# Routing ranks of a mixture-of-experts layer from bfloat16 ones and zeros

## The chip, the cores and the metric

The kernel runs on one core of one Trainium2 chip, as one program in one launch. The metric is the device time of that launch in microseconds (us), the median of several runs. Lower is better. The engines are TensorE (PE in the profile, PEld for its weight loads), VectorE (DVE), ScalarE (ACT), GpSimd (POOL) and SyncE (SP, which here only issues transfers).

## The reference

The input is x, 8 sequences of 512 tokens with 128 channels, so 4096 tokens, all in float32. Three layers follow, each added to x:

```
x = x + 0.5 * ffn(layernorm(x))
x = x + wkv6(layernorm(x))          # a recurrence with a decay per channel
x = x + 0.5 * ffn(layernorm(x))     # the same weights as the first

def ffn(x):
    x = x + attention(layernorm(x, w, b))          # 16 heads of 8 channels
    h = layernorm(x, w2, b2)
    logits = h @ gate_w + gate_b                    # 8 experts
    one_hot = onehot(argmax(logits))
    y = sum over e of one_hot[:, e] * (gelu(h @ w1[e]) @ w2[e])    # hidden size 512
    return x + y
```

Only one expert counts for each token. The kernel therefore sorts the tokens by expert and computes that expert alone.

## The kernel before, in words

The program is a chain of phases. Each is a block in which every engine has its own list of instructions, and between two phases stands a barrier of all engines (`Phase.__exit__`, L63). A feed-forward layer has four phases: the products for queries, keys and values (`qkv_phase`), the attention (`attention_phase`), projection and routing (`project_phase`, the one touched here), and the experts (`expert_phase`). Between the two feed-forward layers stand two phases for the recurrence; at the end the last sum is stored. So `project_phase` runs twice.

`project_phase` walks over 8 slices (SL) of 4 tiles (ST) of 128 tokens. In words, for slice j:

- TensorE: `turn_y(j)` transposes the attention's result (L916), ScalarE copies it to `yT` (L968), `project(j)` multiplies it by `w_proj` (L908).
- VectorE: `add(j)` makes `x1` (L999), `moments_of` and `gather_moments` its mean and variance (L1009, L1017), `variance(j)` adds eps (L1024), `halve(j)` (L1003) updates `x_all`.
- GpSimd: `scale(j)` raises the variance to the power -0.5 (L1162). VectorE: `norm(j)` writes the normalised tokens into `rows` (L1030).
- TensorE: `turn_h(j)` transposes them (L933), ScalarE makes `h2T` (L974), `gate(j)` multiplies by the gate's weights (L924).
- VectorE: `logits`, `greatest`, `equals`, `numbers`, `first`, `choose` (L1037 to L1060) find the first expert with the greatest logit and write a row of 8 zeros and ones per token, `one_hot` (L1060).
- TensorE: `rank(j)` (L941, L943) counts for each token how many tokens before it chose each expert. The first matmul has a triangle of ones as its weights (`below`, 128x128) and all five groups of `one_hot` as its moving operand (40 columns; the fifth group is zero). Four more have a matrix of ones as weights and 32, 24, 16 and 8 columns; each adds the counts of an earlier tile to the later ones, in the same 40 columns of PSUM.
- VectorE: `places(j)` (L1069, L1071) adds the running count of the slices before, `own_places`, `slots` and `whole` (L1076 to L1084) make from it the row to which each token goes.
- GpSimd: `scatter(j)` (L1155) issues four indirect DMAs, one per tile, which write the 128 rows of a tile to their places in DRAM (`sorted`).

These steps are laid out by hand in turns k. In turn k TensorE does `project(k-1)`, `turn_y(k)`, `gate(k-4)`, `turn_h(k-3)`, `rank(k-5)`, in this order. VectorE does `add(k-1)`, `logits(k-4)`, `moments_of(k-1)`, `greatest`, then `places(k-5)`, which waits for the rank of the same turn; after it come `gather_moments(k-1)`, `own_places`, `equals`, `slots`, `variance(k-1)`, `halve`, `numbers`, `whole`, `norm(k-2)`, `first` and `choose(k-4)`. GpSimd does `scale(k-1)` and then `scatter(k-6)`. Engines take their instructions in order, so on GpSimd `scale(5)` of turn 6 stands in front of the first `scatter`, and `scale(6)` and `scale(7)` stand in front of the next two groups of four.

When the last slice has been counted, VectorE stores where each expert's rows end (`pad_row`, L1123), SyncE writes a tile of padding behind each expert's rows (L896), VectorE finds expert and first row of each of 40 tiles of sorted rows (L1124 to L1144), and GpSimd waits for the landing of all 32 scatters. Then comes the barrier. `expert_phase` loads the sorted tiles (L1203) and runs two layers of the expert's weights over each (L1226, L1232, L1239).

All operands of `rank` are float32 before the change. In the trace each of these float32 matmuls shows as two rows for the weight load and two for the matmul.

Of the kernel before, what the change touches and what calls it, by code (L numbers as in the profile page):

```python
# [6 lines left out]
BF16 = mybir.dt.bfloat16  # L7
# [6 lines left out]
P = 128  # L14
# [17 lines left out]
E, HID = 8, 512  # L32
# [5 lines left out]
ST = NT // SL  # L38
# [4 lines left out]
def own(nc, name):  # L43

    return f"{name}_{nc.next_id()}"
# [801 lines left out]
def project_phase(nc, ps, s, x_all, z_all, rows, expert, first_row, xs):  # L847
# [4 lines left out]
    with Phase(nc) as ctx:  # L852
        def sb(name, shape, dt=F32):
            return ctx.enter_context(nc.sbuf_tensor(own(nc, name), shape, dt))

        def sem(name):
            return ctx.semaphore(name)

        def sbs(name, shape, dt=F32):
            return [sb(f"{name}{i}", shape, dt) for i in range(2)]  # L860
# [2 lines left out]
        x1 = [sb(f"x1{i}", [P, ST, P]) for i in range(3)]  # L863
        stats, moments = sb("stats", [P, ST, 6]), sbs("moments", [P, ST, 2])
        power, var, rstd = sb("power", [P, ST]), sbs("var", [P, ST]), sbs("rstd", [P, ST])
        power_set, var_ready, rstd_ready = sem("power_set"), sem("var_ready"), sem("rstd_ready")
        index, base = sb("index", [P, E]), sb("base", [P, E])
        logit, best, equal = sb("logit", [P, ST, E]), sb("best", [P, ST]), sb("equal", [P, ST, E])
        one_hot, place, run = sbs("one_hot", [P, ST + 1, E]), sb("place", [P, ST, E]), sbs("run", [P, E])
        slot_f, slot = sb("slot_f", [P, ST]), sb("slot", [P, NT], I32)  # L870
        total, above, tiles, ends, delta = (sb("total", [P, E]), sb("above", [P, E, NT]), sb("tiles", [P, E]),
                                            sb("ends", [P, E]), sb("delta", [P, E]))
# [11 lines left out]
        psR = [ps[:, 6 + i, 2 * ST * E:(3 * ST + 1) * E] for i in range(2)]  # L884
# [5 lines left out]
        with nc.Block() as block:  # L890
            @block.sync
            def _(sp):
                sp.wait_ge(pads_ready, 1)
                for e in range(E):
                    row = sp.value_load(pad_row[0:1, e:e + 1], min_val=0, max_val=E * (TOK + P) - P)
                    sp.dma_start(xs[ds(row, P), :], s["padding"][:, 0, :]).then_inc(padded, 16)  # L896
                sp.wait_ge(padded, 16 * E)

            @block.tensor
            def _(pe):  # L900
                t = nc.tensor

                def project(j):
                    pe.wait_ge(y_kept, j + 1)
                    if j >= 2:
                        pe.wait_ge(x1_ready, j - 1)
                    for q in range(ST):
                        last = t.matmul(psP[j % 2][:, q * P:(q + 1) * P], yT[j % 2][:, q * P:(q + 1) * P], s["w_proj"][:],  # L908
                                        start=True, stop=True)
                    last.then_inc(projected, 1)  # L910

                def turn_y(j):
                    if j >= 2:
                        pe.wait_ge(y_kept, j - 1)
                    for q in range(ST):
                        last = t.transpose(psY[j % 2][:, q * P:(q + 1) * P], rows[:, j * ST + q, 0:P], s["ident"][:])  # L916
                    last.then_inc(y_turned, 1)

                def gate(j):
                    pe.wait_ge(h_kept, j + 1)  # L920
                    if j >= 2:
                        pe.wait_ge(ranks_read, j - 1)
                    for q in range(ST):
                        last = t.matmul(psL[j % 2][:, q * E:(q + 1) * E], h2T[j % 2][:, q * P:(q + 1) * P], s["gate_w"][:],  # L924
                                        start=True, stop=True)
                    last.then_inc(gated, 1)

                def turn_h(j):
                    pe.wait_ge(normed, j + 1)
                    if j >= 2:  # L930
                        pe.wait_ge(h_kept, j - 1)
                    for q in range(ST):
                        last = t.transpose(psH[j % 2][:, q * P:(q + 1) * P], rows[:, j * ST + q, 0:P], s["ident"][:])  # L933
                    last.then_inc(h_turned, 1)

                def rank(j):


                    hot = one_hot[j % 2][:].rearrange("p t e -> p (t e)")
                    pe.wait_ge(one_hot_ready, j + 1)  # L940
                    t.matmul(psR[j % 2], s["below"][:], hot, start=True, stop=False)  # L941
                    for back in range(1, ST + 1):
                        last = t.matmul(psR[j % 2][:, back * E:], s["ones"][:], hot[:, 0:(ST + 1 - back) * E],  # L943
                                        start=False, stop=(back == ST))
                    last.then_inc(ranked, 1)

                for k in range(SL + 5):
                    if 1 <= k <= SL:
                        project(k - 1)
                    if k < SL:  # L950
                        turn_y(k)
                    if 4 <= k < SL + 4:
                        gate(k - 4)
                    if 3 <= k < SL + 3:
                        turn_h(k - 3)
                    if 5 <= k:
                        rank(k - 5)
# [189 lines left out]
            @block.gpsimd  # L1147
            def _(pool):
                g = nc.gpsimd

                def scatter(j):
                    pool.wait_ge(normed, j + 1)
                    pool.wait_ge(placed, j + 1)
                    for i in range(j * ST, (j + 1) * ST):
                        pool.indirect_dma_start(xs, bass.IndirectOffsetOnAxis(ap=slot[:, i:i + 1], axis=0),  # L1155
                                                rows[:, i, :], None).then_inc(scattered, 16)

                def scale(j):
                    pool.wait_ge(var_ready, j + 1)
                    if j >= 2:  # L1160
                        pool.wait_ge(normed, j - 1)
                    g.tensor_tensor(rstd[j % 2][:], var[j % 2][:], power[:], ALU.pow).then_inc(rstd_ready, 1)  # L1162

                g.memset(power[:], -0.5).then_inc(power_set, 1)
                pool.wait_ge(power_set, 1)
                pool.wait_ge(numbered, 1)
                for k in range(1, SL + 6):
                    if k <= SL:
                        scale(k - 1)
                    if k >= 6:  # L1170
                        scatter(k - 6)
                pool.wait_ge(scattered, 16 * NT)
# [798 lines left out]
def program(nc, d, out):  # L1971
    with Phase(nc) as ctx:
# [15 lines left out]
        def ffn(load=None):  # L1988

            with ExitStack() as inner:  # L1990
                v_all = inner.enter_context(nc.sbuf_tensor(own(nc, "v_all"), [P, NT, H, DK + 1], F32))
                qkv_phase(nc, ps, s, x_all, z_all, v_all, qd, kd, load)
                attention_phase(nc, ps, s, v_all, y_all, qd, kd, load)
            project_phase(nc, ps, s, x_all, z_all, rows, expert, first_row, xs)
            expert_phase(nc, ps, s, expert, first_row, xs, ys)
# [54 lines left out]
```

## Time and profile before

| what | us |
|---|---|
| median of 3 runs | 1562.1 (1561.02 to 1567.3) |
| the profiled execution | 1553.92 |
| its span, first to last instruction | 1552.0 |
| TensorE busy | 1284.2 (83% of the span) |
| VectorE busy | 1082.9 (70%) |
| ScalarE busy | 859.3 (55%) |
| GpSimd busy | 659.1 (42%) |
| first `project_phase`, first instruction to the first load of the experts | 440.4 to 520.2 |
| second one | 1365.4 to 1445.0 |
| mean granted clock of TensorE | 0.871 of 2.4 GHz |

The shares of busy time are means over all phases. To read a change inside one phase, its own stretch has to be cut out; times in the rows are counted from the start of the span. In a list in order of time a row is: start, busy time, engine, line, operation, what it writes and reads, how many instructions it merges, and in brackets how long the engine sat idle before it and what ended that.

### The profile page before, as it was taken

The numbers are of one execution on the slowest core, as the hardware profiler recorded it, in microseconds if no ns is written. First come the engines' busy times: TensorE is split into PE (matmuls) and PEld (weight loads), VectorE is DVE, ScalarE is ACT, GpSimd is POOL, SyncE is SP. The second block draws the span as 40 slices with busy tenths as digits, with TensorE's granted clock in tenths as the row PEclk, the third lists the DMA queues.
The fourth block names the chain that finished last, engine by engine and source line by source line (L and its number), as shares of the span: only waits on it lengthen the run. The fifth ranks groups of instructions, "written<-read, shape, count | busy, mean of one in ns | idle before, by whom it ended". The sixth has DMA issues, their size and how long they took to land. (4 is left out here: it accounts for less than half of the span.)

```text
span 1552.0 us, 39914 instructions
## 1 busy us (share of the span) xinstructions
PE 1284.2 (83%) x12720; PEld 729.3 (47%) x12721; DVE 1082.9 (70%) x1864; ACT 859.3 (55%) x1750; POOL 659.1 (42%) x767
## 2 busy tenths in 40 slices
PE   5499999999978595288789747499999999976693
PEld 3244444444368595135445444234444444376693
DVE  8588888888555233668788758688888888464232
ACT  3178888888831352234334414178888888820451
POOL 4323333333337463355566533323333333337462
PEclk9689999999975797589899958599999999965797
DMA  5513342221001222000000004311111111001124
GB/s 181 152 37 82 91 108 57 54 52 47 16 1 42 60 67 64 14 2 2 3 3 2 3 1 190 83 43 51 48 50 47 50 48 51 7 1 59 53 69 119
DMA packets 81640, 81.93 MB, mean 53 GB/s; under 512 B 16265, under 2 KB 53868, under 8 KB 81536
## 3 DMA queue, kind: packets, MB, share of 16 engines
q1 hardware_dynamic: 72704, 70.01, 16.3%
q0 software_dynamic: 4608, 8.44, 1.6%
q10 hardware_dynamic: 4224, 2.10, 0.5%
q8 instruction: 64, 1.05, 0.3%
q14 instruction: 40, 0.33, 0.1%
HBM read 50.56 MB, written 29.93 MB: 52 GB/s over the span
## 5 line engine op out<-in xcount | busy, mean ns | idle before, releaser
L817 DVE TENSOR_REDUCE maxima<-ps 128x2 f32<-128x1024 f32 x512 | 624.2, 1226 | 91.0 <-PE ps L646 86.4
L799 ACT ACTIVATE probs<-ps 128x512 f32<-128x512 f32 x1024 | 553.2, 593 | 90.4 <-PE ps L673 73.1
L646 PE MATMUL ps<-k_stack,q_stack 62*128 62x512 f32 x1024 | 387.6, 478 | 35.6 <-DMA k_stack<-k_split 24.4
L673 PE MATMUL ps<-q_stack,k_stack 64*128 64x512 f32 x1024 | 392.1, 461 | 0.4
L683 PE MATMUL ps<-probs,v_stack 128*32 128x256 f32 x4096 | 329.0, 393 | 1.1 <-ACT probs L799 1.0
L612 POOL TENSOR_TENSOR inv<-o_rows,minus_one 128x16 f32<-128x16 f32 x64 | 186.0, 2906 | 237.5 <-ACT o_rows L780 237.5
L646 PEld LDWEIGHTS ps<-k_stack,q_stack 62*128 62x128 f32 x1024 | 158.7, 194 | 229.9 <-issue 116.5
L673 PEld LDWEIGHTS ps<-q_stack,k_stack 64*128 64x128 f32 x1024 | 160.1, 187 | 17.0 <-issue 6.8
L683 PEld LDWEIGHTS ps<-probs,v_stack 128*32 128x32 f32 x4096 | 81.1, 108 | 172.6 <-issue 113.1
L1297 POOL DMA_INDIRECT expert_out<-yt,number x80 | 78.3, 979 | 68.1 <-POOL number L1293 34.2
L1274 DVE COPY w_now<-w 128x512 f32 x80 | 34.3, 429 | 85.9 <-issue 42.8
L1255 ACT ACTIVATE xT<-ps,ln_b,ln_w 128x128 f32<-128x128 f32 x80 | 36.6, 457 | 94.4 <-PE ps L1226 94.4
L1232 PE MATMUL ps<-xT,w_now 128*128 128x128 f32 x640 | 88.2, 283 | 0.0
L1239 PE MATMUL ps<-w,hidT 128*128 x640 | 84.5, 276 | 0.0
L1232 PEld LDWEIGHTS ps<-xT,w_now 128*128 128x128 f32 x640 | 80.6, 198 | 0.2
L605 POOL CAST neg_wide<-maxima 128x16 fp32r<-128x16 f32 x64 | 12.6, 196 | 158.7 <-DVE maxima L817 158.7
L1239 PEld LDWEIGHTS ps<-w,hidT 128*128 128x128 f32 x640 | 77.9, 192 | 0.1
L1155 POOL DMA_INDIRECT sorted<-rows,slot x64 | 62.3, 973 | 18.3 <-issue 15.9
L1260 ACT ACTIVATE hidT<-ps 128x512 f32<-128x512 f32 x80 | 47.8, 597 | 36.7 <-PE ps L1232 36.7
L1703 POOL TENSOR_TENSOR r_kx<-r_kx,r_k_factor 128x512 f32<-128x512 f32 x48 | 61.3, 1277 | 12.9 <-PE ps L1881 9.1
L1684 POOL TENSOR_TENSOR r_mixed<-r_shift,zT 128x512 f32<-128x512 f32 x40 | 56.9, 1431 | 18.0 <-DVE r_shift L1560 18.0
L1226 PE MATMUL ps<-ident,xt 128*128 128x128 f32 x80 | 23.3, 292 | 44.2 <-DMA xt<-sorted 44.1
(205 smaller groups left out, 1765.5 us busy)
## 6 DMA issues: line engine op xcount, KB each, us to landing
q_stack<-q_split SPq DMA_DIRECT2D x256, 64.0 KB
k_stack<-k_split SPq DMA_DIRECT2D x512, 32.0 KB
q_split<-q_parts SPq DMA_DIRECT2D x16, 512.0 KB, 2.7
k_split<-k_parts SPq DMA_DIRECT2D x16, 512.0 KB, 3.4
xt<-sorted SPq DMA_DIRECT2D x80, 64.5 KB
w<-in_L_ffn_w SPq DMA_DIRECT2D x16, 256.0 KB, 3.1
rows<-expert_out SPq DMA_DIRECT2D x16, 256.0 KB, 3.3
x_all<-in_L_attn_x SPq DMA_DIRECT2D x8, 256.0 KB, 3.1
```

Of the source, the lines that this page charges most:

```text
L612: g_.tensor_tensor(inv[:], o_rows[:, :, :, DK], minus_one[:], ALU.pow).then_inc(inv_ready, 1)
L646: mm = t.matmul(psS[:, h, :], qs[g][score_rows(h), h // 2, u * P:(u + 1) * P], ks[g][score_rows(h), h // 2, :], start=True, stop=True)
L673: t.matmul(ring("e", u, n), ks[g][half(h), h // 2, u * P:(u + 1) * P], qs[g][half(h), h // 2, :], start=True, stop=True).then_inc(e_ready, 1)
L683: last = t.matmul(psO[VW * h:VW * (h + 1), here], vs[g][:, u, h, :], probs[u % 2][:, h, here], start=(u == 0 and part == 0), stop=(u == TP ...
L799: a.activation(probs[u % 2][:, h, :], ring("e", u, n), ACT.Exp, scale=float(DK) ** -0.5).then_inc(e_read, 1)
L817: v.tensor_reduce(maxima[i][:, :, pair, u:u + 1], psS[:, 2 * pair:2 * pair + 2, :], AX_X, ALU.max, negate=True).then_inc(s_read, 1)
L1155: pool.indirect_dma_start(xs, bass.IndirectOffsetOnAxis(ap=slot[:, i:i + 1], axis=0), rows[:, i, :], None).then_inc(scattered, 16)
L1232: last = t.matmul(psH[o][:, c * P:(c + 1) * P], w1_now[o][:, c * P:(c + 1) * P], xT[o][:], start=True, stop=True)
L1239: last = t.matmul(psY[i][:, 0:P], hidT[i][:, c, :], s["w2"][:, ds(second_expert, 1), c, :], start=(c == 0), stop=(c == HC - 1))
L1297: pool.indirect_dma_start(ys, bass.IndirectOffsetOnAxis(ap=number[out_slot][:], axis=0), yt[out_slot][:], None, bounds_check=TOK - 1, oob_ ...
L1684: g.tensor_tensor(mixed[f][:], shift[f % 2][:], x, ALU.add).then_inc(mixed_ready.sem, 1)
L1703: g.tensor_tensor(dst[:].rearrange("p (k m) -> p k m", m=m), src[:].rearrange("p (k m) -> p k m", m=m), k_factor[l][:].rearrange("p n two ...
```

## The change

`below` and `ones` get copies in bfloat16, `one_hot` becomes bfloat16, and `rank` takes these three. The sums stay float32 in PSUM. All values are zero or one. GpSimd makes the two copies at the start of each `project_phase`, between its memset of `power` and `scale(0)`, and TensorE waits for both before the first rank.

```
+        counters_set = sem("counters_set")
-        one_hot, place, run = sbs("one_hot", [P, ST + 1, E]), sb("place", [P, ST, E]), sbs("run", [P, E])
+        one_hot, place, run = sbs("one_hot", [P, ST + 1, E], BF16), sb("place", [P, ST, E]), sbs("run", [P, E])
+        below, ones = sb("below_16", [P, P], BF16), sb("ones_16", [P, P], BF16)
...
                     pe.wait_ge(one_hot_ready, j + 1)
-                    t.matmul(psR[j % 2], s["below"][:], hot, start=True, stop=False)
+                    if j == 0:
+                        pe.wait_ge(counters_set, 2)
+                    t.matmul(psR[j % 2], below[:], hot, start=True, stop=False)
                     for back in range(1, ST + 1):
-                        last = t.matmul(psR[j % 2][:, back * E:], s["ones"][:], hot[:, 0:(ST + 1 - back) * E],
+                        last = t.matmul(psR[j % 2][:, back * E:], ones[:], hot[:, 0:(ST + 1 - back) * E],
                                         start=False, stop=(back == ST))
...
                 g.memset(power[:], -0.5).then_inc(power_set, 1)
+                g.tensor_copy(below[:], s["below"][:]).then_inc(counters_set, 1)
+                g.tensor_copy(ones[:], s["ones"][:]).then_inc(counters_set, 1)
                 pool.wait_ge(power_set, 1)
```

## Rows read from the trace of the kernel before

**Rows 1.** Waits of 440 to 520: waiting engine, tile, releaser: total, times, longest.

```profile
DVE place L1069 <- PE ps L943: 14.4, 7, 2.5
```

**Rows 2.** Groups of POOL's instructions, 440 to 515: count, busy, mean ns, idle before.

```profile
L1155 POOL DMA_INDIRECT sorted<-rows,slot x32 | 31.2, 975 | 9.2 <-issue 7.9 <-DVE slot L1084 0.6 <-DVE rows L1030 0.3
```

**Rows 3.** POOL in order of time: the last scales and the scatters around them.

```profile
446.61 1.28 POOL L1162 TENSOR_TENSOR rstd<-var,power 128x4 f32<-128x4 f32 x1 [6.08 <-DVE var L1024]
...
469.09 1.50 POOL L1162 TENSOR_TENSOR rstd<-var,power 128x4 f32<-128x4 f32 x1 [5.26 <-DVE var L1024]
470.67 1.21 POOL L1155 DMA_INDIRECT sorted<-rows,slot  x1
...
476.24 1.49 POOL L1162 TENSOR_TENSOR rstd<-var,power 128x4 f32<-128x4 f32 x1 [0.58 <-DVE var L1024]
...
481.73 0.96 POOL L1155 DMA_INDIRECT sorted<-rows,slot  x1 [0.30 <-issue]
482.74 1.28 POOL L1162 TENSOR_TENSOR rstd<-var,power 128x4 f32<-128x4 f32 x1
```

**Rows 4.** The end of the first phase and the start of the experts, in order of time.

```profile
505.12 0.20 DVE L1144 SCALAR_TENSOR_TENSOR first_row<-counts,row_f 128x40 int32<-128x40 f32 x1
...
513.40 0.95 POOL L1155 DMA_INDIRECT sorted<-rows,slot  x1 [0.31 <-issue]
520.16 2.59 SPq L1203 DMA_DIRECT2D xt<-sorted  x3
```

**Rows 5.** TensorE and VectorE in turns 5 and 6, in order of time.

```profile
459.94 0.30 PEld L941 LDWEIGHTS ps<-one_hot,below 128*128 128x128 f32 x2
461.06 1.46 PEld L908 LDWEIGHTS ps<-w_proj,yT 128*128 128x128 f32 x8
...
462.93 1.11 DVE L1030 TENSOR_SCALAR rows<-x,moments,rstd 128x128 f32<-128x128 f32 x4
...
464.81 0.90 PEld L933 LDWEIGHTS ps<-ident,rows 128*128 128x128 f32 x4
465.21 0.19 DVE L1037 TENSOR_TENSOR logit<-ps,gate_b 128x32 f32<-128x32 f32 x1 [0.24 <-PE ps L924]
...
465.70 0.55 PEld L941 LDWEIGHTS ps<-one_hot,below 128*128 128x128 f32 x2
...
468.09 0.19 DVE L1069 TENSOR_TENSOR place<-ps,run 128x32 f32<-128x32 f32 x1 [1.82 <-PE ps L943]
...
468.85 0.16 DVE L1024 TENSOR_SCALAR var<-moments 128x4 f32<-128x4 f32 x1
```

**Rows 6.** VectorE in turn 7 of the first phase: the variance.

```profile
476.00 0.16 DVE L1024 TENSOR_SCALAR var<-moments 128x4 f32<-128x4 f32 x1
```

**Rows 7.** The same places in the second phase, in order of time.

```profile
1393.05 0.19 DVE L1069 TENSOR_TENSOR place<-ps,run 128x32 f32<-128x32 f32 x1 [1.82 <-PE ps L943]
...
1401.20 1.49 POOL L1162 TENSOR_TENSOR rstd<-var,power 128x4 f32<-128x4 f32 x1 [0.70 <-DVE var L1024]
```

**Rows 8.** Groups of POOL's instructions in the whole span.

```profile
L597 POOL COPY v_stack<-v_all 128x144 f32<-128x144 f32 x16 | 4.7, 317 | 8.4 <-PE ps L683 8.3
L612 POOL TENSOR_TENSOR inv<-o_rows,minus_one 128x16 f32<-128x16 f32 x64 | 186.0, 2906 | 237.5 <-ACT o_rows L780 237.5
```

**Rows 9.** Stretches: busy time and count of PE, PEld, DVE, ACT, POOL; clock; DMA.

```profile
440.40:454.40 14.00, 11.87 (x50) 10.47 (x51) 9.43 (x44) 3.42 (x6) 3.42 (x4) 0.50 0.00 1
454.40:461.40 7.00, 6.25 (x57) 6.16 (x57) 6.61 (x33) 2.75 (x4) 2.14 (x2) 0.98 0.01 2
461.40:470.60 9.20, 9.20 (x46) 9.20 (x45) 7.10 (x44) 1.37 (x2) 2.99 (x2) 0.50 0.00 1
...
522.00:526.00 4.00, 3.33 (x15) 3.04 (x16) 0.43 (x1) 2.78 (x5) 0.37 (x2) 0.50 0.21 51
526.00:560.00 34.00, 34.00 (x301) 33.86 (x301) 12.26 (x34) 18.73 (x37) 19.18 (x33) 1.00 0.22 64
```

## The prediction, written before the changed kernel ran

> **What bounds the kernel now.** I began with the table of waits over the first `project_phase`. It holds a tempting line: VectorE waits 14.4 us for the ranks, seven times and up to 2.5 us each [rows 1]. Twice that, for two phases, is 28.8 us, the most the change could be worth. A wait counts only if what it holds up is what ends last, so the next view was the end of the phase. VectorE has finished its tables at 505.32 (505.12 + 0.20), while GpSimd issues its last scatter until 514.35, and the first load of the experts follows at 520.16 [rows 4]. The phase ends with the scatters, and VectorE and TensorE are 9 us early.
>
> So I followed GpSimd backwards. The 32 scatters are busy 31.2 us with 9.2 us of idle in front of them, 7.9 of it "issue", the 0.30 us between one scatter and the next [rows 2]: one scatter per 1.26 us. GpSimd's order from the first scatter on is fixed: 4 scatters, `scale(6)`, 4 scatters, `scale(7)`, 24 scatters. From 470.67 to 514.35 are 43.7 us; 32 x 1.26 = 40.3 plus the two scales, 1.49 and 1.28 [rows 3], is 43.1. Only about 0.6 us is left, and nearly all of it stands in front of `scale(6)`, which waited 0.58 us for VectorE's variance. In front of `scale(7)` the gap is 0.05 us (481.73 + 0.96 to 482.74) [rows 3]. So a rank counts only where it delays the first scatter or makes that gap. All later waits of VectorE for a rank are slack.
>
> What delays the first scatter is `scale(5)`: it starts at 469.09, ends at 470.59, and the scatter starts 0.08 later [rows 3]. It needs `variance(5)` (468.85), which stands on VectorE behind `places(1)`, and that waited 1.82 us for rank(1), until 468.09 [rows 5]. This is the wait that the change can shorten with effect, once per phase.
>
> **The change part by part.**
>
> *The ranks' matmuls.* A rank is now ten rows of weight load and ten of matmul, since each of the five float32 matmuls shows as two. At the clock of 0.50 which the chip grants from 461.40 on [rows 9], rows follow each other every 0.22 us (the four of L933 from 464.81, then L941 at 465.70: 0.89); ten are 2.2, and 0.19 of hand-over brings it to 468.09 - 465.70 = 2.39 [rows 5]. No bfloat16 matmul stands in the trace. Bounds: at worst nothing is saved; in between, five rows at the old pace, 5 x 0.22 + 0.19 = 1.29 us; at best nothing but the hand-over. I take five rows at half the old time, 0.55 + 0.19 = 0.74 us: half the rows, each loading half the bytes.
>
> The FP8 and Floating Point Precision page of the Trainium skill (TensorE Precision Notes) says that a true float32 product takes four passes through the array; the trace shows two rows for each, so the rows may hold two passes each. By that rule a bfloat16 row would cost half a row, which is the value taken.
>
> *Rank(0)* runs at the high clock and occupies TensorE from 459.94 to 461.06, 1.12 us [rows 5]; five rows at the old pace would be 0.56, at half the time 0.28. So everything behind it comes 0.56 to 0.84 us earlier. `turn_h(3)` can't start before `norm(3)` is done at 464.04 (it started at 464.81), which caps the shift at about 0.7. Rank(1) then starts at 465.0 to 465.14 in place of 465.70, and its result is there at 465.75 (half the time per row) or 466.43 (old pace).
>
> *What is late next.* VectorE was ready for `places(1)` at 466.27 (468.09 - 1.82). It had lost 0.24 us in front of `logits(2)` waiting for the gate's matmul [rows 5]; that comes early too, so it is ready at 466.03. With the shorter rows VectorE itself becomes the bound: 468.09 - 466.03 = 2.06 us gained. At the old pace it is 1.66. I take 2.0.
>
> *The gap before scale(6).* The first four scatters now end near 473.65. `variance(6)` stood at 476.00 [rows 6]; it moves by the 2.0 of turn 6 and by rank(2)'s own wait, of the same size, to about 472.2. The gap falls from 0.58 to 0.05, a gain of 0.53.
>
> After this GpSimd has no gap left. A turn costs it 1.5 + 4 x 1.26 = 6.5 us while turns have a scale; VectorE's and TensorE's own turns (TensorE: 24 float32 rows x 0.22 + 0.55 = 5.8) are shorter. Whatever else the ranks save, it waits for GpSimd.
>
> *The two copies.* 128x128 elements each, on GpSimd. The nearest row is a copy of 128x144 at 0.317 us; the dearest small operation is the 128x16 power at 2.906 [rows 8]. Two cost 0.6, at the very worst 5.8 us. They stand in front of `scale(0)`, before which GpSimd idles 6.08 us [rows 3], so even the worst is hidden. Without that cover they would cost what they take. The wait added on TensorE stands before rank(0), 19 us after the phase began; the next rank and `project(5)` are queued behind it, and it is met long before. VectorE writes 32 columns of bfloat16 in place of float32: between no change and 0.1 us less for each, off the path as well. I put all these at zero.
>
> *The second phase* shows the same picture: 1.82 us of waiting for rank(1) and 0.70 us in front of `scale(6)` [rows 7]. Sum: 2.0 + 0.53 + 2.0 + 0.65 = 5.2 us. The profiled execution of 1553.9 us would become 1548.7; it lies 8.2 us below the median of 1562.1, from which I forecast 1556.9. With only 1.66 per turn and half the gaps it is 3.9, with 2.1 each and both gaps 5.4; with other small effects the forecast's own range is 1555.5 to 1558.5. All of it is 0.33%, under the 0.5% that a measurement of this kernel can tell from no change.
>
> **The rivals.**
>
> *Nothing gained* (1562). The bfloat16 rows run no shorter in sum than the float32 ones, for instance because each matmul now drains before the next one starts: a row of load lasts 0.33 us by itself (0.55 for two that start 0.22 apart [rows 5]); with its matmul behind it, estimated at 0.45 together, five make 2.25, about what ten make now. Against it: the float32 rows of one group do overlap.
>
> *The clock falls earlier* (about 1558.5). TensorE had the high clock from 454.4 to 461.4 and the low one before and after [rows 9], while it was busy nearly all the time. Less work in rank(0) could end that stretch at 460. Then rank(0) at the low clock takes 0.55 to 1.1 us in place of 1.12, `project(5)` 1.83 in place of 1.46 [rows 5], and rank(1) comes later: about 1.2 us gained before the first scatter in place of 2.0. Sum 2 x 1.2 + 1.2 = 3.6.
> The page TensorE: Matmul & The Clock Gate of the Trainium skill (Part 4) says that transposes don't count as work of the array in the way matmuls do. By that rule the eight transposes of a turn weigh more once the ranks shrink, which speaks for this rival. The trace has both clocks with the same mix of transposes, so it does not settle it.
>
> *The waits count at face value* (1562.1 - 28.8 = 1533.3). It needs the scatters to follow TensorE's pace. Against it: GpSimd's list has no idle to give back [rows 2, 3].
>
> *Slower.* TensorE ends its part of the phase 10 us or more earlier, so it idles longer before the experts. There the clock is 0.50 for the first 4 us and then 1.00 [rows 9]. If a longer pause made that low stretch as long as the one at the start of this phase, 14 us [rows 9], 10 us more would run at half pace: 5 us lost per phase, 10 in all, against 5.2 gained: 1566.9. It shows as slower than the 0.5% from 6.5 us lost per phase, that is 13 us more at the low clock: 1570. Against it: the pause is already longer than 15 us (from before 505.3, where VectorE has used the last rank, to 520.16 [rows 4]) and the clock starts at its lower level in either case.
>
> **How the numbers follow.** The forecast has 0.70, the earlier fall of the clock 0.11, nothing gained 0.09, face value 0.05, slower 0.05. The likeliest gives 1556.9. The range of 1553 to 1564 takes in the first three and the runs' own scatter (1561.0 to 1567.3 before). Faster by over 0.5% means below 1554.3: face value, and 0.07 from the forecast's tail, 0.12. Slower by over 0.5% means above 1569.9: most of the slower rival and some scatter, 0.04. Within: 0.84.
>
> **What would show it.** In the changed profile: five weight loads per rank in place of ten, and VectorE's wait for the rank in turn 6 near zero; GpSimd's first scatter of each phase 2.0 us earlier after the phase's first instruction (30.3 before: 470.67 - 440.4), 4 scatters, `scale(6)` with no gap, and the last scatter 2.5 us earlier; the copies done before 442; the stretch from last scatter to first load still 5.8 us; VectorE done with its tables some 20 us before the last scatter in place of 9. The prediction is wrong if a phase shortens by more than 3.5 us (then something other than GpSimd's list bounds it) or by less than 1.

## The result, and the profile after

The changed kernel takes 1550.47 us (median of 6 runs, 1549.27 to 1552.04), against 1562.5 for the kernel before on the same chip (6 runs, 1559.67 to 1567.3): ratio 0.992, interval 0.990 to 0.9941. The forecast was 1556.9 with a range of 1553 to 1564; the gain is 12 us, not 5.2. The profiled execution took 1549.46 us, with a span of 1547.4.

The first lines of its page (busy time, share, instructions) give the size of the edit: 80 matmuls and 80 weight loads fewer than before in all, five per rank, 16 ranks.

```profile
span 1547.4 us, 39760 instructions
PE 1241.1 (80%) x12640; PEld 686.8 (44%) x12641; DVE 1083.2 (70%) x1864; ACT 859.2 (56%) x1750; POOL 659.8 (43%) x771
```

The table of waits for 440 to 520 us (engine and tile that wait, releaser: total, times, longest), answering to [rows 1]:

```profile
POOL rstd L1167 <- DVE var L1029: 18.5, 6, 5.6
POOL sorted L1160 <- issue: 9.2, 31, 0.3
DVE place L1074 <- PE ps L948: 1.9, 2, 1.7
```

VectorE's 14.4 us in front of the ranks are 1.9 us. GpSimd in order of time, answering to [rows 3] (start, duration, idle in brackets; this phase starts at 441.60):

```profile
441.72 0.29 POOL L1170 CAST below<-below 128x128 bf16<-128x128 f32 x1
441.95 0.31 POOL L1171 CAST ones<-ones 128x128 bf16<-128x128 f32 x1
447.86 1.28 POOL L1167 TENSOR_TENSOR rstd<-var,power 128x4 f32<-128x4 f32 x1 [5.59 <-DVE var L1029]
...
467.69 1.50 POOL L1167 TENSOR_TENSOR rstd<-var,power 128x4 f32<-128x4 f32 x1 [3.04 <-DVE var L1029]
469.27 1.22 POOL L1160 DMA_INDIRECT sorted<-rows,slot  x1
...
473.31 0.98 POOL L1160 DMA_INDIRECT sorted<-rows,slot  x1 [0.30 <-issue]
474.32 1.05 POOL L1167 TENSOR_TENSOR rstd<-var,power 128x4 f32<-128x4 f32 x1
475.56 1.03 POOL L1160 DMA_INDIRECT sorted<-rows,slot  x1 [0.19 <-issue]
...
480.68 1.04 POOL L1167 TENSOR_TENSOR rstd<-var,power 128x4 f32<-128x4 f32 x1
...
511.09 0.95 POOL L1160 DMA_INDIRECT sorted<-rows,slot  x1 [0.30 <-issue]
```

The copies are over at 442.26, in front of an idle of 5.59 us. The first scatter comes 27.67 us after the phase's start (30.3 before), `scale(6)` follows the fourth scatter without a gap, and the last scatter ends 70.44 after the start (before, [rows 3, 4]: 514.35 - 440.35 = 74.0). GpSimd's list did what was forecast, and more: 3.6 us per phase instead of 2.6.

And yet the phase isn't shorter. From its first barrier to its last it takes 79.8 us, 79.0 in the profile before. The end of the phase, VectorE and SyncE's queue in order of time, answering to [rows 4]:

```profile
493.33 16.28 SPq L899 DMA_DIRECT2D sorted<-padding  x4
...
494.89 0.20 DVE L1149 SCALAR_TENSOR_TENSOR first_row<-counts,row_f 128x40 int32<-128x40 f32 x1
...
515.21 3.90 SPq L899 DMA_DIRECT2D sorted<-padding  x4
522.17 0.37 SPq L1210 DMA_DIRECT2D xt<-sorted  x1
```

VectorE is done 17 us before the last scatter's end (9 before). But SyncE's eight padding stores, each a register load and a small DMA, go out from 493.33 to 519.11: 25.8 us, and now they end the phase. The experts' first load follows them by 3.1 us; it is 10.1 behind the last scatter, where 5.8 was expected. So two questions were open: what slows SyncE, and where 12 us come from if this phase gives nothing in these two profiles. Their record names no chip, and they may come from two: before, the eight padding stores took 8.7 us, in the profile after 25.8.

### The profile page after: what moved, and what is told of

Read it like the earlier page. It is cut to its first block and busy times, and to the rows that moved or that the text cites. A ratio compares the mean times of both kernels' runs of the same rounds, so it can differ in the third digit from the quotient of the medians.

```text
span 1547.4 us, 39760 instructions
## 1 busy us (share of the span) xinstructions
PE 1241.1 (80%) x12640; PEld 686.8 (44%) x12641; DVE 1083.2 (70%) x1864; ACT 859.2 (56%) x1750; POOL 659.8 (43%) x771
## 5 line engine op out<-in xcount | busy, mean ns | idle before, releaser
L683 PEld LDWEIGHTS ps<-probs,v_stack 128*32 128x32 f32 x4096 | 81.1, 108 | 173.1 <-issue 113.1
L1304 POOL DMA_INDIRECT expert_out<-yt,number x80 | 78.3, 979 | 69.1 <-issue 40.5
L1239 PEld LDWEIGHTS ps<-xT,w_now 128*128 128x128 f32 x640 | 81.1, 199 | 0.0
L605 POOL CAST neg_wide<-maxima 128x16 fp32r<-128x16 f32 x64 | 12.5, 196 | 159.1 <-DVE maxima L817 159.1
L1710 POOL TENSOR_TENSOR r_kx<-r_kx,r_k_factor 128x512 f32<-128x512 f32 x48 | 60.3, 1257 | 13.6 <-PE ps L1888 9.8
```

Source lines behind the costliest of these rows:

```text
L683: last = t.matmul(psO[VW * h:VW * (h + 1), here], vs[g][:, u, h, :], probs[u % 2][:, h, here], start=(u == 0 and part == 0), stop=(u == TP ...
L1239: last = t.matmul(psH[o][:, c * P:(c + 1) * P], w1_now[o][:, c * P:(c + 1) * P], xT[o][:], start=True, stop=True)
L1304: pool.indirect_dma_start(ys, bass.IndirectOffsetOnAxis(ap=number[out_slot][:], axis=0), yt[out_slot][:], None, bounds_check=TOK - 1, oob_ ...
L1710: g.tensor_tensor(dst[:].rearrange("p (k m) -> p k m", m=m), src[:].rearrange("p (k m) -> p k m", m=m), k_factor[l][:].rearrange("p n two ...
```

## The experiments

Times are medians; "before" is the kernel before on the same chip. Four chips, A to D, took part. The runs of a chip share their runs of before (on D there are two sets). Phase times are of one profiled execution of each kernel, from barrier to barrier: R1 and R2 are the two routing phases, rec is the recurrence, which the edit doesn't touch.

```
kernel             chip    time    before  ratio [95%]               R1    R2    rec
before (profile)    -                                               79.0  78.9  277.2
after (profile)     -                                               79.8  79.2  271.0
before_again        A    1549.42  1550.55  0.9999 [0.9982, 1.0015]  78.4  78.9  273.1
after_again         A    1539.05           0.9932 [0.9909, 0.9955]  74.4  75.9  269.0
casts_only          A    1547.64           0.9980 [0.9963, 0.9997]  78.9  75.9  272.4
pads_on_act         A    1543.71           0.9961 [0.9940, 0.9982]  75.4  75.7  272.4
early_ranks         B    1552.72  1561.83  0.9947 [0.9930, 0.9964]  83.8  81.1  270.0
late_ranks          B    1555.89           0.9960 [0.9946, 0.9973]  85.0  84.1  271.4
first_layer         B    1554.01           0.9947 [0.9929, 0.9966]  81.2  84.9  271.6
rows_kept           B    1553.14           0.9946 [0.9924, 0.9967]  81.3  80.6  274.8
before_b            C    1561.98  1561.15  1.0005 [0.9989, 1.0022]  85.2  84.1  276.0
after_b             C    1550.42           0.9940 [0.9921, 0.9959]  80.2  80.3  269.7
ranks_twice         C    1559.92           0.9997 [0.9980, 1.0014]  83.3  82.8  275.3
scatter_first       C    1544.00           0.9896 [0.9876, 0.9915]  77.0  76.4  270.3
after_c             D    1546.40  1560.96  0.9909 [0.9891, 0.9928]  77.9  77.5  271.7
rows_kept_b         D    1553.38           0.9959 [0.9943, 0.9975]  81.0  80.2  273.2
scatter_first_f32   D    1550.08           0.9926 [0.9898, 0.9955]  79.9  78.2  273.9
scatters_last       D    1579.55           (one run)                93.5  93.8  270.4
rows_first          D    1567.84  1561.89  1.0039 [1.0020, 1.0059]  87.9  87.5  274.4
both_moves          D    1538.95           0.9853 [0.9828, 0.9878]  74.0  74.1  272.3
```

### The two kernels again, on three chips

No edit. 

> The kernel before, unchanged. Open after the result: the one profiled execution before (1553.9 us) lies 6 us under all its timed runs (1559.7 to 1567.3), while that of the changed kernel (1549.5) lies among its own (1549.3 to 1552.0). Theory A (SyncE's pace): in most executions SyncE runs its instructions behind the scatters at some 0.7 us each, as in the changed kernel's profile, and in the kernel before, where the eight padding stores are issued 10 us later, this holds back the end of the phase; the one profiled execution had no such stretch. It expects 1560 to 1566, and in this profile SyncE's eight stores spread over well more than 9 us, ending after the last scatter, some 5 to 9 us more from last scatter to first load (5.8 before). Theory B (the clock): the runs differ in the recurrence, whose TensorE clock goes up and down; it expects both routing phases as before (73.9 us to the last scatter's end, 5.8 us behind) and the recurrence phase (277.2 us before) longer by 5 or more.

> The changed kernel, unchanged. Ratio 0.992 again, 1549 to 1552 us. From first instruction to the end of the last scatter 70.4 and 70.6 us (73.9 before). Theory A: the padding stores are slow again (about 25 us for eight) and end at about the last scatter's end plus 7. Theory B: the recurrence phase is near 271 us as in its first profile, against 277 before, in each execution.

> The kernel before once more, for its profile beside the changed kernel's on one chip. Two kinds of chip have been seen: one without standstills (kernel before 1550, routing phases 79 us) and two with (1562). Theory S (standstills behind the scatters): on a chip of the second kind SyncE takes 0.7 us for each of its small instructions and VectorE or TensorE stands for several us from about 23 us behind the first scatter on; the phases of the kernel before then take 84 to 87 us and those of the changed one 80 to 81. On a chip of the first kind: 79 and 75.4. The theory that the surplus over my forecast lies outside these phases expects them to differ by 3.5 us each on either chip.

> The changed kernel beside it. Theory S: on a chip with standstills routing phases of 80 to 81 us, and a gain of 10 to 12 us in all; on a chip without, 75.4 us and 7 us of gain in these phases. The other phases should agree within the run-to-run scatter of the recurrence (269 to 277 us seen).

> The changed kernel again, the base of the runs beside it. It should stand 10 to 13 us below the kernel before, with the recurrence at 269 to 272 us, if the chip has standstills (routing phases of 80 us, padding stores that end 77 us into the phase); 10 to 12 us below if it has none (routing phases of 75 us).

The gain is there on every chip: 11.5 us on A (1550.55 - 1539.05), 10.7 on C, 14.6 on D. (On A both kernels were expected 10 us higher.) But chip A is another place: the kernel before takes 1550 us there, and 1561 to 1562 on the others. SyncE's queue shows it, in the changed kernel on chip A

```profile
489.93 8.86 SPq L899 DMA_DIRECT2D sorted<-padding  x8
516.82 12.66 SPq L1210 DMA_DIRECT2D xt<-sorted  x7
```

and the same kernel on chip C:

```profile
493.10 25.66 SPq L899 DMA_DIRECT2D sorted<-padding  x8
521.72 6.47 SPq L1210 DMA_DIRECT2D xt<-sorted  x6
```

On C, engines come to a standstill late in the phase. In the kernel before, on C, VectorE in order of time:

```profile
490.84 0.19 DVE L1042 TENSOR_REDUCE best<-logit 128x4 f32<-128x32 f32 x1
498.66 0.19 DVE L1069 TENSOR_TENSOR place<-ps,run 128x32 f32<-128x32 f32 x1 [7.63 <-remote]
```

and TensorE's weight loads there:

```profile
491.54 1.83 PEld L943 LDWEIGHTS ps<-one_hot,ones 128*128 128x128 f32 x8
499.03 1.14 PEld L924 LDWEIGHTS ps<-gate_w,h2T 128*128 128x128 f32 x5 [5.67 <-issue]
```

The rank's last load ends at 493.37, and VectorE takes its result only at 498.66: it has stood for 7.63 us, TensorE for 5.67, and neither has work of the other to wait for in most of that time. This is what is called a standstill below. A second one of 8.0 us follows, and GpSimd then waits 4.8 us for `slot`. The last scatter ends 78.3 us after the phase's start (74.0 in the profile before) and the last padding store 83.0. The phase takes 85.2 us instead of 79. In every profile of chips B to D but scatters_last, the phase ends 2.2 to 2.4 us behind the last padding store, so there it is the stores that end it. The profile of before, on which the forecast rests, shows nothing of it. Its time, 1553.9, lies below all six timed runs of its kernel beside the changed one, but inside those of chip A (1544 to 1556).

### Copies alone, and the stores on another engine (chip A)

casts_only keeps copies and wait, but ranks float32:

```
-  one_hot = sbs("one_hot", [P, ST + 1, E], BF16) ...
+  one_hot = sbs("one_hot", [P, ST + 1, E]) ...
-  t.matmul(psR[j % 2], below[:], hot, ...)        # and ones[:]
+  t.matmul(psR[j % 2], s["below"][:], hot, ...)   # and s["ones"][:]
```

> The two bfloat16 copies on GpSimd and TensorE's wait are there, but the ranks still take the float32 operands and one_hot is float32. If the gain lies in the ranks' matmuls (all theories): as before, ratio 1.000 within 0.002, 73.9 us to the last scatter's end in each routing phase. If the gain came from a shifted layout of code or of the buffers: below 0.996.

The copies cost nothing: 2.9 us faster than before, an interval that just leaves out 1. The format is worth 8.6 us beside them (1547.64 - 1539.05). In R2 the float32 ranks reach the bfloat16 result (75.9); there the high clock lasted 20.5 us.

pads_on_act moves the padding loop (wait, eight register loads and stores) from SyncE to the end of ScalarE's list:

> The changed kernel with its eight padding stores per phase issued by ScalarE, which has nothing left to do, in place of SyncE. Theory A (SyncE's slow pace holds the end back, 4 us per phase): if only SyncE's sequencer is slowed, the stores take 9 us for eight, the stretch from last scatter to first load falls from 10.1 and 9.3 to 5.8 us, and the time falls by 7 to 8 us against the changed kernel (ratio 0.987). If any issuing engine is slowed while scatters run, the stores take some 25 us here too and the time is that of the changed kernel (0.992). Theory B says nothing of it: same as the changed kernel.

On A, where SyncE is not slow, it gains nothing and is 4.7 us slower than after_again; in the profiles 1.0 us of that is in R1 and 3.4 in the recurrence.

### Which ranks count (chip B)

```
+  narrow = [j <= 2 for j in range(SL)]   # early_ranks; late_ranks: j > 2; first_layer: by layer
+  one_hot = [(hot16 if narrow[j] else hot32)[j % 2] for j in range(SL)]
```

The weights (`below`, `ones`) go with it.

> Ranks 0, 1 and 2 of each phase take bfloat16 operands, ranks 3 to 7 float32. Theory G (GpSimd's list is the bound; a rank counts only until the first scatter and scale(6)): first scatter at 27.7 us into the phase and last scatter's end at 70.5, as with all eight, and the phase 75.4 us against 79.0; 7 us less in all, ratio 0.9955. Theory W (the waits for all ranks count): three of eight ranks, so 3/8 of the whole gain of 11.5 us, 4.3 us, ratio 0.997, last scatter's end near 72.7.

> Ranks 3 to 7 take bfloat16 operands, ranks 0 to 2 float32. Theory G: first scatter at 30.3, last scatter's end at 74.0, phases 78.9, nothing gained, ratio 1.000, though VectorE's waits for five ranks are gone. Theory W: 5/8 of the gain, 7 us, ratio 0.995. If a part of the gain lies outside the routing phases and comes with shorter lists of instructions, this kernel has 5/8 of that part: 2 to 3 us.

> All eight ranks in bfloat16 in the first feed-forward layer only. Theory G: half of the gain of the routing phases, 3.5 us (first routing phase 75.4, second 78.9), ratio 0.9977; the phases between them as before. If more than that shows, some of it lies in the phases between the two.

early_ranks has the first scatter at 27.6 to 28.0 us, late_ranks at 30.3, as the theory of GpSimd's list asks. By that theory late_ranks should be worth nothing; it is worth 5.9 us. But no gain shows in its routing phases: they take 85.0 and 84.1 us, those of the kernel before on chip C 85.2 and 84.1 (chip B has no profile of before). VectorE has its tables at 59.8 us, 15 earlier than there, and the scatters end at 73.9 instead of 78.3. SyncE's queue shows what ends the phase:

```profile
499.98 24.20 SPq L902 DMA_DIRECT2D sorted<-padding  x8
527.14 2.59 SPq L1214 DMA_DIRECT2D xt<-sorted  x3
```

The stores go out 14 us earlier than in before_b and take 24.2 us instead of 10.4, so they end at the same distance from the start, 83 us. What differs lies outside: the recurrence takes 271.4 us (276.0 in before_b), the phase ahead of it 40.3 (42.1).

early_ranks is worth 9.1 us. Its phases take 83.8 and 81.1 us in spite of the earlier scatter: its float32 ranks run into standstills (VectorE 9.5 and 3.9 us in the first phase, 6.1 and 12.9 in the second), and VectorE's tables come at 71 and 73 us. With all eight ranks in bfloat16 on C they come at 54 and 55, and the phases take 80.2 and 80.3. So on such a chip the later ranks shorten the phase only on top of the earlier ones. This compares one profile each, on two chips. first_layer shows both kernels' phases in one execution: 81.2 us, then 84.9 with standstills of 7.6 and 8.1 us.

### TensorE's list, and work beside the scatters

rows_kept (B) and rows_kept_b (D) have 40 more rows of float32 behind the last rank, as many as the edit removed; rows_first (D) has the same ahead of the first transpose; ranks_twice (C) does each rank's five matmuls twice.

```
+  for filler in range(20):                # rows_kept: after the loop; rows_first: before it
+      t.matmul(psH[0][:, 0:E], s["ones"][:], s["ident"][:, 0:E], start=True, stop=True)

+  for again in range(2):                  # ranks_twice: around the matmuls of rank(j)
```

> The changed kernel with 20 float32 matmuls of 8 columns behind the last rank of each phase, where TensorE has nothing left to do: as many rows in its list as before the change (40 fewer loads and 40 fewer matmuls per phase are put back), 4.5 us of work 15 us before the phase ends. If the gain beyond the routing phases (some 4 us of the 11.5) comes from the length or place of TensorE's list: 7 us gained, ratio 0.9955. If not: as the changed kernel, 0.9925. The routing phases stay at 75.4 in both.

> Each bfloat16 rank is computed twice, so TensorE's work for ranks is doubled (ten bfloat16 matmuls of 8 to 40 columns in place of five). Theory G (GpSimd's list is the bound): 0.2 to 0.3 us later at the first scatter at most, last scatter's end within 0.5 us of the changed kernel, time the same within 1 us. If each us of rank still counted: 16 x 0.25 = 4 us slower.

> The changed kernel with 20 float32 filler matmuls of 8 columns behind the last rank, so that TensorE's list is about as long as in the kernel before, here timed again beside the changed kernel on one chip. Theory L (the recurrence, which the change doesn't touch, is shorter by 4 us because TensorE's instruction list ahead of it is shorter): recurrence 273 to 277 us, 3 to 5 us slower than the changed kernel in all. Theory C (the recurrence's time varies by chip and execution alone): recurrence 269 to 272 us and within 1 us of the changed kernel.

> The changed kernel with the same 20 float32 filler matmuls as in rows_kept, but ahead of TensorE's first transpose of the routing phase, where nothing else is late yet: TensorE's list ahead of the recurrence is as long as in the kernel before, and no filler runs beside the scatters. Theory L (the list's length alone sets the recurrence's time): recurrence 273 to 277 us; each routing phase 3 to 5 us longer than in the changed kernel, since the fillers' 4.5 us stand ahead of everything, and the whole is 8 to 13 us above the changed kernel, 1555 to 1560 us on a chip with standstills. Theory C: recurrence 269 to 272 us.

rows_first, the busy line of its page:

```profile
PE 1259.5 (80%) x12720; PEld 704.5 (45%) x12721; DVE 1086.0 (69%) x1864; ACT 859.1 (55%) x1750; POOL 657.6 (42%) x771
```

TensorE has as many instructions as before the change, and the recurrence is back at 274.4. The routing phases, though, are 87.9 and 87.5 us, some 10 above after_c where 3 to 5 were expected: the fillers' loads take 8.6 us instead of 4.5 and the first scatter comes at 36.1 us.

Over all 20 profiles: with a TensorE list of the old length (9) it takes 272.4 to 277.2 us, mean 274.5; with a shorter one (11) 269.0 to 272.4, mean 270.9. Chance alone doesn't sort them like this, but part of it is the clock: five of the short ones had 201 to 205 us at the high clock, none of the long ones over 198. Among those with 198 us the means are 274.2 (6) and 271.8 (5). In the pair on chip D the difference was 1.5 only. So a list of the old length goes with an untouched recurrence that is slower by 2 to 4 us. It is not in proportion to the rows: early_ranks, with 15 loads and matmuls per phase fewer in place of 40, has 270.0. Why is not shown.

ranks_twice cost 9.5 us against after_b, where at most 1 to 4 were expected: by the profiles 5.6 in the recurrence, 5.6 in the routing phases, where VectorE stands for 10.1 and 13.6 us at a time. rows_kept_b cost 7.0 against after_c, of which 5.8 in the routing phases, although its fillers block nobody (8.8 us of loads behind the last rank). In these two pairs work on TensorE beside the scatters isn't free. rows_kept on B doesn't show it: its ratio, 0.9946, is that of after_b, 0.9940, within the interval.

### Do the scatters bring the standstills? (chip D)

```
-  for k in range(1, SL + 6):
-      if k <= SL:
-          scale(k - 1)
-      if k >= 6:
-          scatter(k - 6)
+  for k in range(SL):
+      scale(k)
+  pool.wait_ge(pads_ready, 1)
+  for k in range(SL):
+      scatter(k)
```

> The changed kernel, but GpSimd does all eight scales first and waits until VectorE has handed over the padding rows before the first of the 32 scatters. Theory S (the standstills of VectorE, TensorE and SyncE come from the scatters, 22 us or more after the first one): VectorE has no idle time over 3 us in the phase and is done near 60 us after its start, the eight padding stores, which go out in the scatters' first 10 us, take 8 to 9 us, and the phase is about 60 + 42 + 6 = 108 us. Theory T (they come at a time or place of the phase, about 55 us after its start, whatever GpSimd does): VectorE or TensorE stands 5 to 8 us there, or the padding stores take over 15 us.

SyncE's queue in scatters_last, in order of time:

```profile
491.04 9.22 SPq L899 DMA_DIRECT2D sorted<-padding  x8
536.54 3.69 SPq L1210 DMA_DIRECT2D xt<-sorted  x4
```

and its GpSimd:

```profile
490.29 1.30 POOL L1160 DMA_INDIRECT sorted<-rows,slot  x1 [10.99 <-DVE pad_row L1128]
491.90 0.96 POOL L1160 DMA_INDIRECT sorted<-rows,slot  x1 [0.30 <-issue]
```

The stores go out at nearly the same distance from the phase's start as in after_c (48.8 us, there 50.6), but inside the scatters' first 10 us, and take 9.2 us instead of 25.1. VectorE and TensorE have next to nothing left to do by then, so this shows it for SyncE alone, in one execution: its slow stretch follows the scatters, not the place in the phase. The first late idle stretches of VectorE over 3 us, wherever they were seen, begin 19 to 27 us after the first scatter, which fits. My estimate of the phase, 108 us, was bad (93.5 and 93.8): VectorE handed over the padding rows at 48, not 60. What inside the chip does it, and why chip A hasn't got it, stays open.

### Two versions that beat both

scatter_first (C) and scatter_first_f32 (D, float32 ranks) let GpSimd scatter before it scales; both_moves (D) adds ScalarE's stores.

```
   for k in range(1, SL + 6):
+      if k >= 6:
+          scatter(k - 6)
       if k <= SL:
           scale(k - 1)
-      if k >= 6:
-          scatter(k - 6)
```

> The changed kernel with GpSimd's list in another order: scatter(k-6) in front of scale(k-1) in place of behind it. Theory G: scatter(0) can start when slot(0) is there, some 22 us into the phase, and fills the 3 us that GpSimd idles in front of scale(5); the first scatter comes at 22 in place of 27.7, the last one ends 3 us earlier (67.5 in place of 70.5), 3 us per phase, 6 us in all on a chip without standstills. If something else bounds the phase (landing of the data, TensorE), nothing is gained.

> The kernel before (float32 ranks) with one change: GpSimd issues the four scatters of a group before it does the next scale. Theory G (the phase ends with GpSimd's list, which begins when rank(0) has been read): the first scatter comes 3.5 to 4 us earlier than in the kernel before (26.5 us after the phase's start instead of 30.3) and the kernel is 5 to 8 us faster than the kernel before, so that the ranks' format is then worth less (4 to 7 us) on top. Rival: the float32 ranks then stand between scale and scatter (VectorE waits for them) and the gaps move into the scatters' list: within 2 us of the kernel before.

> The changed kernel with GpSimd's scatters of a group ahead of the next scale (scatter_first) and the padding stores issued by ScalarE (pads_on_act). On a chip with standstills, if SyncE's slow padding stores end the phase: first scatter 23.7 us, last scatter's end 67.5 us after the phase's start, padding stores over by 60 us, phase 72 to 73 us, 1536 to 1541 us in all, 4 to 8 us below scatter_first's 1544. Rival: ScalarE's padding stores take as long as SyncE's there, and the time stays at 1543 to 1546 us. On a chip without standstills it is 1532 to 1538 us either way.

With the order changed the first scatter of scatter_first and scatter_first_f32 comes at 23.6 to 23.9 us, with either format, since it no longer stands behind `scale(5)`: 6.6 us earlier than before (3.5 to 4 expected with float32; 22 us expected with bfloat16). That alone gives the kernel before 10.9 us. With float32 ranks VectorE again stands 4 to 5 us late in the phase, and the last scatter ends at 70.4 to 71.8, with bfloat16 ranks at 67.4 to 67.8. scatter_first is 6.4 us below after_b; both_moves is 1538.95, 7.5 below after_c and 23 below the kernel before. In it ScalarE's queue needs nearly as long for the stores as SyncE did,

```profile
492.57 20.76 ACTq L976 DMA_DIRECT2D sorted<-padding  x8
```

and they end 71.8 us after the phase's start (74.2 to 74.8 in scatter_first; 60 expected). So the rival, that ScalarE is as slow there, is right but for 1.4 us. What the move of the stores is worth by itself is not shown: both_moves ran on D and scatter_first on C, and against the changed kernel of their own chip their phases are shorter by nearly as much (3.9 and 3.4 us; 3.2 and 3.9).

## Why the prediction was wrong

*That only the first scatter and the gap before `scale(6)` count.* Right for GpSimd's list: VectorE's tables are ready 11.5 us earlier (505.32 - 440.35 against 495.09 - 441.60), and 3.6 us of that arrive at the last scatter. On chip A it is right for the phase too, which is 4.0 and 3.0 us shorter, in each case within 0.1 us of what the last scatter is earlier. The view used, GpSimd backwards from the last scatter, was the right one for that.

*The term 2.0* (first scatter) measured 2.6 in the first pair of profiles and 2.1 in both phases on C. `places(1)` waits for no rank any more (at 466.69, with no idle in front of it): TensorE's weight loads in turns 5 and 6, answering to [rows 5],

```profile
460.77 0.10 PEld L946 LDWEIGHTS ps<-one_hot,below 128*128 128x128 bf16 x1
460.88 0.17 PEld L948 LDWEIGHTS ps<-one_hot,ones 128*128 128x128 bf16 x4
460.98 0.97 PEld L911 LDWEIGHTS ps<-w_proj,yT 128*128 128x128 f32 x8
...
465.30 0.10 PEld L946 LDWEIGHTS ps<-one_hot,below 128*128 128x128 bf16 x1
465.41 0.18 PEld L948 LDWEIGHTS ps<-one_hot,ones 128*128 128x128 bf16 x4
465.52 0.97 PEld L911 LDWEIGHTS ps<-w_proj,yT 128*128 128x128 f32 x8
```

show rank(0) holding TensorE for 0.21 us (460.77 to 460.98; 1.12 before, 0.28 taken), rank(1) for 0.22 (2.20 before, 0.55 taken). At the high clock a bfloat16 load takes 0.04 us and a float32 row 0.11 (1.12 / 10), so 0.37 of a row where a half was taken; the rest of rank(1) is the clock.
The Trainium skill, in TensorE: Matmul & The Clock Gate (Weight-path perf modes), has a fast weight load that is on for 128 weights of a type other than float32. The trace agrees: 0.04 against 0.11 us.

*That the clock holds or falls earlier.* It is up longer. Stretches of the changed kernel, answering to [rows 9] (busy time and count of PE, PEld, DVE, ACT, POOL; clock; DMA share; GB/s):

```profile
455.50:462.50 7.00, 5.15 (x48) 4.80 (x47) 6.97 (x37) 2.24 (x4) 2.28 (x2) 1.00 0.01 2
462.50:471.50 9.00, 6.05 (x55) 5.44 (x54) 8.93 (x53) 2.75 (x4) 4.92 (x4) 1.00 0.03 9
```

1.00 where the kernel before had 0.50 from 461.4 on. In 13 routing phases with float32 ranks in the early turns the high clock lasted 6.8 us, in two of them longer (13.7, 20.5); in all 27 with bfloat16 there it lasted 13.7 to 23.9 in sum, in most of them in two stretches with 3 to 7 us at the low level between. So the rival had the wrong sign, and in the profile shown rank(1), `project(5)` and the transposes of turn 6 ran at the high clock as well. The clock alone can give the 2.6: in R2 of casts_only, with float32 ranks and 20.5 us of high clock, the first scatter came at 27.6 us too. So how much of this term is the shorter rank and how much the clock is not separated.

*The term 0.53* (the list behind the first scatter) measured 0.9: 42.8 us (469.27 to 512.04) against 43.7. The two scales between scatters took 1.05 and 1.04 us instead of 1.49 and 1.28, which I had left as they were, and the 0.58 us gap is gone.

*That nothing outside the routing phases changes* was not said but used: the sum has only their terms and puts everything else at nothing, without a reason. This step failed. late_ranks shows it: its routing phases are as long as those of the kernel before on chip C (85.0 and 84.1 us against 85.2 and 84.1), and yet it is 5.9 us faster. The recurrence took 274.5 us in the mean with the old list, 270.9 with a shorter one; in the pairs on one chip it gave 4.1 us on A and 6.3 on C.

*"Whatever else the ranks save, it waits for GpSimd"; "All later waits of VectorE for a rank are slack".* On chips with standstills this failed as well, in part. With the early ranks in bfloat16, float32 later ranks leave VectorE's tables at 71 to 73 us and the phases at 83.8 and 81.1; with all in bfloat16 VectorE is ready 26 us after the first scatter instead of 45, and the phases take 80.2 and 80.3. By themselves the later ranks gained nothing in the phase (late_ranks). What bounds the phase there is the padding stores, which the prediction gave no time at all. Per phase on C: 85.2 and 84.1 became 80.2 and 80.3, 4.4 on average, of which 2.6 was forecast.

In sum, with the phases of C and the mean of the recurrence: 8.8 + 3.6 = 12.4; measured 10.7 on C, 12 in the result and 14.6 on D. The pair of profiles on C differs by more, 16.1 us, since its execution of before, 1566.1, lay 5.0 us above the median of the chip's other runs: 8.8 in routing, 6.3 in the recurrence, 1.8 in the phase ahead of it, while the first experts' phase was 2.9 longer.

*The base.* The profiled execution lay 8.2 us below the median. I carried that over as an offset. It was the sign that the profile lacked something which costs about 5.7 us per phase on chip C (84.7 against 79.0), and which the change acts on. Its phases (79.0 and 78.9), its fast stores and the lack of standstills are those of chip A. The range, which reached down to 1553 for runs' scatter, left it out.

*The rivals.* Nothing gained, slower, and face value (1533.3) are all refuted. Of 12.5 us of waiting saved per phase 3.0 to 5.0 arrived at the phase's end (A and C).

*What would make it wrong* was named as a phase shorter by more than 3.5 us, "something other than GpSimd's list bounds it". On chip C, with 5.0 and 3.8 us, that came true, and there the padding stores bound it. The 4.0 us of chip A's first phase are GpSimd's list all the same.

## What to carry to other kernels

Where the profiled execution is faster than every timed run, the profile lacks a cost that the median has; find out on which phase before you call its waits slack. A wait off the bounding list is slack only while the list stays the bound: on three chips here the padding stores ended the phase. Time the phases that the edit doesn't touch as well; about a third of this gain lay there. And look at the order of the bounding engine's own list first: moving one line gave 10.9 us where the new format of 16 ranks gave 14.6 on the same chip.

## What the runs showed of the hardware that I had not expected

- Beside a long run of indirect DMAs issued by GpSimd, on three of four chips, from 18 to 27 us after the first one other engines slow or stop: VectorE and TensorE for 3 to 14 us at a time, and SyncE needs 22 to 27 us for eight stores that begin 22 to 30 us after it and take 9 inside the first 10 us (scatters_last) or on chip A, ScalarE 20.8 (7.8 on chip A). No run separates the causes for this.
- Five bfloat16 matmuls of 8 to 40 columns hold TensorE for 0.21 us, their float32 forms for 1.12 at the same clock.
- Bfloat16 ranks in the early turns went with more time at the high clock, not less, even where each was done twice (17.1 us in both phases of ranks_twice).
- The length of TensorE's list in the routing phase goes with the time of a phase that the edit doesn't touch, by 2 to 4 us.
